# A fused feed-forward, attention, feed-forward kernel: where each attention batch begins on TensorE and ScalarE, and who sums the first batch's expert outputs

## What is computed

```
x = x + 0.5 * ffn(layernorm(x))
x = x + attention(layernorm(x))
x = x + 0.5 * ffn(layernorm(x))

attention(x):            # 256 tokens a sequence, 16 heads of 8 numbers
    q, k, v = x @ w_q.T, x @ w_k.T, x @ w_v.T
    q, k = rotate(q), rotate(k)                  # (re*cos - im*sin, re*sin + im*cos)
    att = softmax(q @ k.T / sqrt(8))
    return (att @ v) @ w_o.T

ffn(x):                  # 8 experts, hidden 512, each token uses its best 2
    logits = x @ Wg + bg;  top 2;  scores = softmax(top 2)
    y_e = gelu(x @ W1[e] + b1[e]) @ W2[e] + b2[e]
    return layernorm(x + sum over the 2 of scores * y_e) * gamma + beta
```

## Time and profile before

| | us |
|---|---|
| median of 3 runs | 440.87 |
| lowest, highest | 436.80, 441.81 |
| the profiled execution's own time | 441.32 |
| its span | 439.5 |
| PE busy | 386.4 (88%) |
| DVE busy | 327.0 (74%) |
| ACT busy | 260.4 (59%) |
| POOL busy | 228.9 (52%) |

### The profile page before, as it was taken

How to read it: one execution, slowest core, us unless ns; L and a number is a source line. 1 busy time by engine, 2 the same in 40 slices (tenths; PEclk the granted TensorE clock), 3 DMA queues, 4 the chain that set the end, 5 groups by cost and what they waited for, 6 DMA issues and landing times.

```text
span 439.5 us, 10056 instructions
## 1 busy us (share of the span) xinstructions
PE 386.4 (88%) x3076; PEld 310.7 (71%) x3076; DVE 327.0 (74%) x1078; ACT 260.4 (59%) x525; POOL 228.9 (52%) x293
## 2 busy tenths in 40 slices
PE   4889899998899998989899999999899799999920
PEld 3556588998799875666666667676588699998820
DVE  4667765555776787788899999877557955568995
ACT  1445667765566546577676767675776466675600
POOL 4378875787745353325143543516146768445551
PEclk9655999999999997999999999999999999999975
DMA  9911832123113008980000000001202222252321
GB/s 258 341 44 53 247 83 72 56 62 98 49 48 86 20 26 276 318 274 25 2 24 16 12 15 14 26 7 39 54 26 63 65 64 61 60 147 62 115 78 55
DMA packets 33202, 37.79 MB, mean 86 GB/s; under 512 B 5504, under 2 KB 28032, under 8 KB 32752
## 3 DMA queue, kind: packets, MB, share of 16 engines
q1 hardware_dynamic: 28144, 27.36, 21.0%
q0 software_dynamic: 4544, 9.35, 6.3%
q10 hardware_dynamic: 464, 0.45, 0.5%
HBM read 26.71 MB, written 20.36 MB: 107 GB/s over the span
## 4 chain that ended last, share of the span: by engine, by line
PE 66%; DVE 8%; POOL 8%; issue 7%; ACT 5%; DMA 4%; POOLq 0%; SPq 0%; ACTq 0%; DVEq 0%
PE ps L1028 7%; PE ps L833 6%; PE ps L819 6%; PE ps L806 5%; PE ps L834 4%; PE ps L894 4%; PE ps L939 4%; PE ps L808 3%; PE ps L807 3%; PE ps L676 3%; POOL sorted_x L509 2%; POOL sorted_x L512 2%; PE ps L919 2%; PE ps L838 2%; PE ps L1037 2%
## 5 line engine op out<-in xcount | busy, mean ns | idle before, releaser
L1325 ACT ACTIVATE stage<-ps 128x512 f32<-128x512 f32 x78 | 46.7, 598 | 66.7 <-PE ps L808 66.7
L1909 DVE TENSOR_REDUCE ring_lo<-ps 128x4 fp32r<-128x1024 f32 x64 | 77.6, 1216 | 9.2 <-PE ps L928 8.7
L1381 ACT ACTIVATE stage<-ps 128x1024 f32<-128x1024 f32 x64 | 65.5, 1024 | 18.9 <-PE ps L939 18.3
L833 PE MATMUL ps<-w_hl,bg_hi 128*128 x234 | 64.4, 344 | 1.7 <-DVE stage L1810 1.7
L1802 DVE TENSOR_TENSOR ring_hi<-ps,bg_hi 128x512 fp32r<-128x512 f32 x78 | 53.8, 690 | 15.9 <-ACT bg_hi L1332 15.8
L834 PE MATMUL ps<-w_hl,ring_hi 128*128 x312 | 60.6, 235 | 0.0
L543 POOL DMA_INDIRECT expert_y<-stage x39 | 38.5, 986 | 36.0 <-DVE stage L1810 32.6
L1796 DVE TENSOR_TENSOR bx<-ps,bx 128x128 fp32r<-128x128 f32 x78 | 22.5, 289 | 45.5 <-ACT bx L1307 39.2
L543 POOL DMA_INDIRECT expert_y<-stage,arena x39 | 38.9, 996 | 32.8 <-DVE stage L1810 28.5
L509 POOL DMA_INDIRECT sorted_x<-rows,place_at x32 | 31.9, 998 | 44.8 <-DVE place_at L1617 32.3
L834 PEld LDWEIGHTS ps<-w_hl,ring_hi 128*128 128x128 f32 x312 | 53.9, 191 | 0.0
(11 more groups left out here) (192 smaller groups left out, 950.7 us busy)
## 6 DMA issues: line engine op xcount, KB each, us to landing
sorted_x<-fill SPq DMA_DIRECT2D x8, 1096.5 KB, 16.6
stage<-w SPq DMA_DIRECT2D x16, 256.0 KB, 6.6
stage<-sorted_x SPq DMA_DIRECT2D x39, 64.5 KB, 1.8
arena<-sorted_x SPq DMA_DIRECT2D x39, 64.5 KB, 1.8
y_got<-expert_y SPq DMA_DIRECT2D x16, 128.0 KB, 2.5
stage<-expert_y SPq DMA_DIRECT2D x16, 128.0 KB, 2.6
x_tok<-x SPq DMA_DIRECT2D x4, 256.0 KB, 5.5
sorted_x<-rows,place_at POOLq DMA_INDIRECT x64, 2.3
```

Source lines behind the costliest of these rows:

```text
L833: pe.matmul(both, bg_hi[:, s, c, :], w, start=(c == 0), stop=False, skip_group_check=True)
L1325: act.activation(g_full[:, s, :], ps[:, H_BANK, :], ACT.Gelu).then_inc(g_done, 1)
L1381: act.activation(prob[:, 2 * v:2 * v + 2, :], ps[:, at:at + 2, :], ACT.Exp, scale=SCALE)\
L1909: vec.tensor_reduce(shift_v[:, t, :, 24].rearrange("p (r g j) -> p r j g", r=2, g=2)[:, pair, 2 * jp:2 * jp + 2, :], ps[:, at:at + 2, :].r ...
```

## The change

There are three parts.

Attention, on TensorE: step 0 of a batch (from batch 1 on) is taken apart. `turned_step` issues its four turned scores alone, then comes the weighing of the batch before, and behind it `scores_step` with the four plain scores. The three unread products of step 0 and their place are gone. The weighing waits for the first placed group's copy (`qk4_ready`, 4b+5), since it writes the bank that this copy reads; the plain scores wait for the second one.

Attention, on ScalarE and DVE: the copy of placed group 1 moves from the end of batch b to behind the first exponentials of batch b+1. The high part of the rotated rows of batches 2 to 7 is now made by ScalarE (`rotated_high`), behind the exponentials of step 6, instead of by DVE.

First list: `POOL_SUMS` is 1. Batch 0's weighted sum is formed by DVE in slot 21, its statistics stay in slot 22; POOL forms batch 1's sum in slot 18 instead of 20, and takes the reciprocal roots one slot earlier.

```diff
--- before.py
+++ after.py
@@ -59,7 +59,7 @@
 SCHED_AT = tuple(sum(SCHED_STEPS[:k]) for k in range(4))
 GATE_STEPS = 5
 PLACES = 4
-POOL_SUMS = 0
+POOL_SUMS = 1
 
 CONSTS = dict(bg=EXPERTS, iota8=EXPERTS, iota=SLOTS, round=ORDERS[0], room=EXPERTS, step=ORDERS[1], prow=1,
               gamma=D, beta=D, eye=P, wg=EXPERTS, ones_at=1)
@@ -555,12 +555,10 @@
                     gp.wait_ge(halved, 2)
                 if 12 <= i < 12 + GROUPS:
                     add_beta(0, i - 12)
-                if i == 19:
-                    weighted_sums(0)
-                if i == 20:
+                if i == 18:
                     weighted_sums(1)
-                if 21 <= i < 23:
-                    post_rstd_of(i - 21)
+                if 20 <= i < 22:
+                    post_rstd_of(i - 20)
                 if i == 24:
                     att_rstd(0)
                 if i == 26:
@@ -984,9 +982,6 @@
 
 
                 q = 1 - p
-                if v == 0:
-                    pe.wait_ge(exp_done, STEPS * b + v + 1)
-                    keep_busy(EXP_BANK, 3)
                 if scores_next:
                     scores_free(b + 1, v)
                 if b == 0 and v == 1:
@@ -1001,6 +996,19 @@
                 if scores_next:
                     scores_part(q, v, 1, 2 * (v % MAX_BUF)).then_inc(s_filled, 1)
 
+            def turned_step(b, p):
+
+                pe.wait_ge(qs_ready, 2 * b + 1)
+                pe.wait_ge(exp_done, STEPS * b + 1)
+                scores_t_part(p, 0, 0)
+                scores_t_part(p, 0, 1).then_inc(t_filled, 1)
+
+            def scores_step(b, q):
+
+                scores_free(b, 0)
+                scores_part(q, 0, 0, 0)
+                scores_part(q, 0, 1, 0).then_inc(s_filled, 1)
+
             def place_shifted(b, p, pair, bank=M0):
 
                 pe.wait_ge(max_done, SU * b + 4 * pair + 4 + MAX_BUF)
@@ -1055,11 +1063,15 @@
 
                 q, last = 1 - p, not place_next
                 if b:
-                    step(b, p, 0, place_next)
+                    turned_step(b, p)
                 if last:
                     pe.wait_ge(v_ready, BATCH)
+                elif b:
+                    pe.wait_ge(qk4_ready, 4 * b + 5)
                 if tail:
                     weigh(b - 1, q, 1)
+                if b and place_next:
+                    scores_step(b + 1, q)
                 if place_next:
                     place(b + 1, q, 2, M0)
                 step(b, p, 1, place_next)
@@ -1363,6 +1375,10 @@
                                ps[:, bank, 0:SEQ].rearrange("p (t h c) -> p t h c", t=BT, h=HEADS),
                                ACT.Copy).then_inc(v_ready, 1)
 
+            def rotated_high(b, p):
+                act.wait_ge(rot_sum, b + 1)
+                act.activation(rot_hi[:, p, :, :], rot, ACT.Copy).then_inc(rot_hi_done, 1)
+
             def copy_placed(b, p, g, bank):
 
 
@@ -1393,6 +1409,8 @@
             def batch(b, p, tail=True, place_next=True, project_next=True):
                 q = 1 - p
                 exps(b, 0)
+                if b and place_next:
+                    copy_placed(b + 1, q, 1, M0)
                 if tail:
                     copy_weighed(b - 1, 1)
                 if place_next:
@@ -1419,6 +1437,8 @@
                     for s in range(YB):
                         act.wait_ge(y_scattered[s], scattered_of(0, SLOTS, s))
                 exps(b, 6)
+                if project_next:
+                    rotated_high(b + 2, p)
                 copy_weighed(b, 0)
                 if place_next:
                     copy_values(b + 1, q)
@@ -1430,7 +1450,6 @@
                     act.activation(act_pad[:, :], neg_half[:, 0:1], ACT.Gelu)
                 if project_next:
                     copy_placed(b + 2, p, 0, M1)
-                    copy_placed(b + 2, p, 1, M0)
 
             def split_sel(half):
                 act.wait_ge(att_loaded, 32)
@@ -1898,8 +1917,9 @@
                 if not (isinstance(b, int) and b == 0):
                     vec.wait_ge(rot_ready, b)
                 vec.tensor_tensor(rot, t_cos, t_sin, ALU.add).then_inc(rot_sum, 1)
-                vec.wait_ge(rot_sum, b + 1)
-                vec.tensor_copy(rot_hi[:, p, :, :], rot).then_inc(rot_hi_done, 1)
+                if b < 2:
+                    vec.wait_ge(rot_sum, b + 1)
+                    vec.tensor_copy(rot_hi[:, p, :, :], rot).then_inc(rot_hi_done, 1)
 
             def maxima(b, *us):
                 for u in us:
@@ -1997,8 +2017,12 @@
                     list_blocks(1, first_part=False)
                 if s == 10:
                     shares(0)
-                if 22 <= s < 24:
-                    combine(s - 22, apply_part=False)
+                if s == 21:
+                    combine(0, stats_part=False, apply_part=False)
+                if s == 22:
+                    combine(0, sum_part=False, stats_part=True, apply_part=False)
+                if s == 23:
+                    combine(1, apply_part=False)
                 if s == 24:
                     combine(0, sum_part=False)
                 if s == 25:
```

## The result

Timed side by side on one chip, eight executions of each: the changed kernel takes 443.2 us (440.6 to 446.2), the kernel before 440.9 (436.8 to 443.1). The ratio is 1.010, 95% interval 1.005 to 1.015: **slower by about 1%**, where 434.0 us were forecast. The profiled execution took 442.3 us (span 440.4), against 441.3 (span 439.5).

A forecast was written before the change was run, and what follows sets the result against it. The prediction took TensorE (66% of the chain of waits), with DVE nearly full beside it in attention, as the bound: 441.3 - 4.7 (start of batches) - 2.6 (first list), rounding nothing, = 434.0 us, range 430.5 to 438.2.

The forecast's parts named there:

- the rival of free overlap: Start of a batch: four scores of one kind overlap with themselves, so splitting costs nothing; 431.4 us, chance 0.12.
- the row of four alone: Batch 7's start in the profile: four turned scores issued alone take 0.43 us, the value the forecast took.
- the rule that the forecast set it against: TensorE packing rule: products on different 32-row groups run at the same time; the forecast read it as making the split free.
- it can follow a gain of 1.7 us a batch: DVE in attention: 1.29 us idle plus 0.43 of work removed lets it follow TensorE's 0.64 gain a batch.
- Cost nothing: Rounding moved to ScalarE: the low part ends at 261.2, TensorE asks at 261.40, so no charge, 0.2 us of cover left.
- the 3.3 reckoned: Fall of TensorE's clock in batch 0's slice, 165 to 176 us: 3.3 us lost, taken as the most per fall.
- the fifth rival: Attention: without the unread products the clock falls at starts of batches, up to 3.3 us each; 443.9 to 457 us, chance 0.07.
- 443.9, for three falls: Time if the clock falls at three batch starts without the unread products: 434.0 + 9.9 us.
- By it this change is safe while its gaps stay as short as now: TensorE in attention: by the rule that idleness lowers the clock, no new falls while gaps stay short.
- Granted 1.00 in all batches but 0: Attention: TensorE's granted clock stays full in every batch except batch 0, given as a sign of the forecast.
- the landing of batch 1's load: First list: 2.5 us from issue to landing, batch 1 there at about 104.4, its sum on POOL from 104.4 to 107.1.

The follow-up runs named there:

- i1_cast: The changed kernel with only the rounding of the rotated rows back on VectorE: median 435.2 us against 440.7 for the kernel before, ratio 0.988.
- e2_rot: The kernel before with only the rounding of the rotated rows moved to ScalarE: median 471.3 us against 470.1 for the kernel before, ratio 1.007.
- f4_short: The changed kernel with GpSimd subtracting only 16 of 256 columns from batch 2 on: median 433.8 us against 439.8 for the kernel before, ratio 0.990.
- h3_order: The changed kernel with VectorE's statistics ahead of the gating and the last batch's rounding on VectorE: 437.6 us against 439.9 for the kernel before, ratio 0.994.
- e4_keep: The changed kernel with the three unread products back ahead of the turned scores: median 469.7 us against 470.1 for the kernel before, ratio 1.002.
- e1_list: The kernel before with the change of the first list alone: median 467.9 us against 470.1 for the kernel before, ratio 1.000.
- i2_fill: The changed kernel with two unread products in TensorE's wait ahead of placing group 3, from batch 3 on: 437.8 us against 440.7 before, ratio 0.996.
- g0_cast: The changed kernel with only the rounding back on VectorE, on a slower chip: median 468.2 us against 476.5 for the kernel before, ratio 0.983.

## Why the prediction was wrong

**Part 1, start of the batch: right in its mechanism, wrong in what it is worth.** The turned scores lead the weighing by 0.49 (0.43 to 0.55 forecast), step 1 comes 0.73 earlier. The four plain scores alone take 0.43 (243.05 to 243.48), so the rival of free overlap has fallen. But its condition was misread: the four products of one kind lie on two groups of rows, two on each, and the pairs follow each other at 0.22 us whether the other kind is there or not (the rows of step 1). Products on different rows do run together, and that makes 0.43 for four and 0.44 for eight; the row of four alone agrees with the rule that the forecast set it against. The step that failed is "it can follow a gain of 1.7 us a batch". VectorE's 1.29 us of idle were taken for slack. Only 0.65 of them are waits, these two in the batch, from the kernel before's timeline:

```profile
252.27 0.19 DVE L1606 TENSOR_TENSOR ranks<-picks,ps 128x32 f32<-128x32 f32 x1 [0.29 <-ACT yt L1391]
...
254.91 0.69 DVE L1889 TENSOR_TENSOR arena<-ps,rope_sb 128x512 f32<-128x512 f32 x1 [0.36 <-PE ps L894]
```

and they stand at 0.30 and 0.36 when TensorE comes earlier (batch 5 of the changed kernel); the rest lies between instructions that wait for one another on VectorE itself. So batches 3 to 5 gain nothing (20.5 in i1_cast), batches 1, 2, 6 and 7 gain 0.7: from 136.5 to 133.8 over the seven, 2.7 us in place of 4.7.

**A wait was overlooked.** Ahead of placing group 3 TensorE waits for VectorE's division, which has no idle mark in the trace of before because it ended 0.05 us earlier. Whatever TensorE gained earlier in a VectorE-set batch had to come out there. It did, as 0.84 us of idle with the hold and 0.41 to 0.44 in i1_cast.

**Part 2, the rounding: "Cost nothing" is the step that turned the sign, most of it by way of the clock.** The low part arrived in time; the forecast looked at who waits for GpSimd's subtraction and not at what runs beside it. 0.43 saved, 0.86 lost in a hold: +0.4 us in a batch, shown by e2_rot, f4_short and h3_order from three sides. (Batch 4 of the first profile has a hold and takes 20.4 all the same, behind the fall in batch 3; why is open.) By itself this is 1.2 us at most, too little to turn a gain into a loss. Attention takes 139.6 in the changed kernel and 133.8 with the rounding back: of these 5.8 us some 0.8 are the hold in batches 3 and 5, and about 5 are the two falls of the clock.

**The clock: the fifth rival had the sign and the kind, not the place.** Its chance was 0.07, tied to the unread products; e2_rot and e4_keep show falls with them in place. A fall cost 2.5 us, near the 3.3 reckoned. That its 443.9, for three falls, lies near the measured 443.2 is luck: the profile has two, and other terms failed too. "By it this change is safe while its gaps stay as short as now" failed twice: the gaps did not stay as short (up to 0.86 us in batches 3 to 5 of the changed kernel, 0.49 before), and in e4_keep and h3_order, where they did, the clock fell too. Ahead of each fall in batches 3 to 5 of the changed kernel TensorE had stood idle, 0.84 us for the division and 0.48 a little later. That goes together and is not a rule: of the seven batches with both idles in the three profiles of the changed kernel, three had no fall; e1_list had an idle of 0.84 in batch 4 without one; and in e4_keep and h3_order the falls came behind 0.25 and 0.5 alone, idles that the kernel before has too. That the hold makes falls likelier is what the mean clocks say (0.935 and 0.938 with it, 0.950 and 0.955 in i1_cast and f4_short without; but h3_order has 0.943); how it does is shown in part, by i2_fill. "Granted 1.00 in all batches but 0" failed.

**Part 3, the list: right in three of four distances.** 2.5, 2.4, 2.3 and 3.7 against 2.7, 2.4, 2.4 and 2.6 forecast; VectorE had no wait for the load. The list as a whole stood 1.24 us earlier in this trace (101.16 against 102.40), so the forecast's times have to be read 1.24 earlier: VectorE came for the root at 109.3, as reckoned, and GpSimd's root, reckoned for 109.2, was there at 110.28. The term that was too small is the landing of batch 1's load, taken as 2.5 us from issue: it took up to 4.0, and GpSimd began the sum 3.05 us behind the first of the five blocks instead of 2.0. In h3_order it was 2.0, and the fourth distance 2.6. The gain was up to 2.7 where the root was ready and mostly 0.9 to 1.7 where not; why the load lands late in some executions is open.

**The sum.** The profiled execution took 442.3 us, 8.3 more than forecast. Attention has 7.8 of them (3.1 longer instead of 4.7 shorter), the second list 1.0, and the stages ahead of attention gave 0.5 more than the forecast asked of them (3.1 instead of 2.6). The two parts without the rounding gained 2.7 in attention and, where the root was ready, up to 2.7 in the list, and the median of i1_cast is 5.5 below that of the kernel before on its chip. The forecast of 434.0 was nearly that of the change without its rounding part, and came near it partly by luck, since attention was reckoned at 4.7.

**Open:** why a fall comes across the end of batch 6 in the changed kernel, where the idle ahead of it is as before; how much idle the clock bears (e2_rot has a fall after 0.25, 0.21 and 0.49 us of idle); and why the fall in batch 3 stays, shorter, with the idle filled.

## What to carry to other kernels

Idle time of a nearly full engine is slack only where its timeline shows a wait for the engine that gets faster; list those waits, and look for semaphores with no idle mark that are met by less than the gain. When an operation moves from one engine to another, look at what the next operation in its chain will run beside: a GpSimd operation that reads SBUF cost nothing here beside a VectorE maximum from PSUM, MAX8 or statistics with one input, and its whole rest beside a two-input operation or a conversion. Try the parts of such a change one by one: here two were worth 1.2% and the third took it all back, more of it by the clock than by its own cost.

## What the runs showed of the hardware

A two-column VectorE subtraction (0.16 us) and a four-column conversion (0.17 us) took 1.05 and 1.03 us beside GpSimd's 128x512 subtraction and ended within 0.03 us of it, while MAX8, the search for its indices and the statistics kept their times beside it. The granted clock fell to the lower level of 1.2 GHz within the attention although TensorE was busy for about 90% of each batch: idles of 0.84 and 0.48 us came ahead in the changed kernel, and the same two idles stood in three other batches without a fall. And one kernel's time differed by 8% between chips (440 and 476 us for the kernel before). The profiles of i1_cast and g0_cast, one kernel on two chips, have spans of 436.0 and 463.6 us: batches 1, 2, 4 and 5 are the same, and most of the difference lies in the head (8.6 us), the first list (6.8) and the second (10.8).
